# A decoder layer on one core: a reordered boundary between attention and feed-forward, additions at the turn's head, and x normalised by ScalarE

## The reference

```python
x = x + attn(layernorm(x))                    # 8 query heads, 2 key/value heads, rope, causal
x = x + wkv(layernorm(x), ctx)                # decayed running sums over time, per channel
x = x + h_bitlinear(silu(gate) * up, w_down)  # gate, up = h_bitlinear(layernorm(x), w)
# attn: softmax(q k^T / sqrt(32)) v, mixed per head with a second ("geometric") softmax
#       of products of the first 3 channels' projections, then @ Wo
# wkv:  y_t = (sum_s w^(t-s) e^k_s v_s + e^(u+k_t) v_t) / (the same without v)
# h_bitlinear: Hadamard transform, per-token 8-bit rounding, ternary weights, matmul
```

## Time and profile before

| | us |
|---|---|
| median of 3 runs (431.3, 433.52, 435.24) | 433.52 |
| the profiled execution | 436.28 |
| its span, first to last instruction | 434.5 |
| rounds 4 to 15 of attention | 67 to 231 |
| first z of pair 0, of pair 1, of pair 3 | 258.33, 278.02, 319.94 |

### The profile page before, as it was taken

The page is one execution under the profiler, slowest core; times in us unless marked ns, Lnnn a source line. Parts: engine busy times, 40 slices in busy tenths (PEclk is TensorE's granted clock), DMA queues, the critical chain, the costliest instruction groups (busy, mean ns, idle before and its releaser), DMA issues. The chain is left out here.

```text
span 434.5 us, 7685 instructions
## 1 busy us (share of the span) xinstructions
PE 359.6 (83%) x2338; PEld 252.4 (58%) x2338; DVE 341.9 (79%) x936; ACT 269.2 (62%) x534; POOL 130.6 (30%) x160
## 2 busy tenths in 40 slices
PE   1877899889888898979888666588888999989794
PEld 1644555565555655555555344476767777778573
DVE  4473989888899888988897647788879889897732
ACT  1242767668776687757687535766848576675542
POOL 1201232334324343232341223432424343332310
PEclk9965999999999999998999978698999999999999
DMA  8960003000000000000000000000000000000001
GB/s 220 296 217 2 0 2 109 14 14 14 2 12 14 14 13 2 12 14 14 14 2 13 14 0 0 2 2 0 14 13 13 12 14 12 26 1 26 14 24 37
DMA packets 13711, 13.43 MB, mean 31 GB/s; under 512 B 2007, under 2 KB 12887, under 8 KB 13543
## 3 DMA queue, kind: packets, MB, share of 16 engines
q1 hardware_dynamic: 13671, 12.94, 10.0%
HBM read 10.84 MB, written 2.10 MB: 30 GB/s over the span
## 5 line engine op out<-in xcount | busy, mean ns | idle before, releaser
L412 POOL TENSOR_TENSOR c_h_lo<-c_hb,c_h_hi 128x512 fp32r<-128x512 f32 x32 | 41.0, 1280 | 72.9 <-ACT c_h_hi L464 67.6
L700 PE MATMUL wide<-had,c_h_hi 128*128 128x512 f32 x128 | 54.1, 423 | 8.1 <-ACT c_q2T L475 8.1
L700 PE MATMUL wide<-had,c_h_lo 128*128 128x512 f32 x128 | 51.2, 400 | 0.0
L927 PE MATMUL bank<-w_o,a_att 128*128 128x256 f32 x128 | 33.5, 407 | 13.1 <-DVE a_att L1226 12.4
L685 PE MATMUL wide<-c_q_T,w_tern_all 128*128 128x256 bf16 x256 | 37.2, 287 | 7.7 <-DVE c_hh L1038 6.1
L457 ACT ACTIVATE c_sl<-c_z 128x512 f32<-128x512 f32 x32 | 20.1, 629 | 29.8 <-DVE c_z L1029 29.7
L390 POOL TENSOR_TENSOR b_ev_in<-b_e_in,b_vT 128x256 f32<-128x256 f32 x16 | 19.9, 1242 | 50.0 <-ACT b_e_in L518 50.0
L927 PEld LDWEIGHTS bank<-w_o,a_att 128*128 128x128 f32 x128 | 24.2, 198 | 18.1 <-DVE a_att L1226 14.4
L685 PEld LDWEIGHTS wide<-c_q_T,w_tern_all 128*128 128x128 bf16 x256 | 24.2, 103 | 18.0 <-DVE c_hh L1038 8.0
L378 POOL TENSOR_TENSOR a_qk<-a_rot_c,a_rot_s 128x320 f32<-128x320 f32 x16 | 15.2, 949 | 62.5 <-DVE a_rot_s L1172 62.5
L700 PEld LDWEIGHTS wide<-had,c_h_hi 128*128 128x128 f32 x128 | 24.6, 193 | 15.0 <-issue 10.2
(11 more groups left out here) (186 smaller groups left out, 1003.0 us busy)
## 6 DMA issues: line engine op xcount, KB each, us to landing
x_res<-in_x SPq DMA_DIRECT2D x4, 512.0 KB, 7.8
b_vT<-in_ctxT SPq DMA_DIRECT2D x16, 128.0 KB, 2.3
out<-c_yo SPq DMA_DIRECT2D x16, 128.0 KB, 1.7
w_raw_all<-in_wg SPq DMA_DIRECT2D x1, 1024.0 KB, 9.2
w_raw_all<-in_wu SPq DMA_DIRECT2D x1, 1024.0 KB, 11.3
w_raw_all<-in_wd SPq DMA_DIRECT2D x1, 1024.0 KB, 13.7
had_f<-in_h SPq DMA_DIRECT2D x1, 1024.0 KB, 4.9
w_o_raw<-in_Wo SPq DMA_DIRECT2D x4, 128.0 KB, 6.1
```

What stands on the lines that cost most here:

```text
L412: nc.gpsimd.tensor_tensor(h_lo[p][:, j::FQ, :], hb[j % 2][:, :].rearrange("c (m t) -> c m t", m=2), h_hi[p][:, j::FQ, :].bitcast(F32), ALU ...
L700: mm = nc.tensor.matmul(wide[:, 1 + i, m * 512:(m + 1) * 512], a[p][:, j + FQ * m, i * P:(i + 1) * P], had512[:, j, :], start=(j == 0 and ...
L927: mm = nc.tensor.matmul(wo_o, att[p][:, i * P:i * P + P], w_o[:, i, :], start=(i == 0), stop=(i == REP - 1))
```

## The change

- `woven` runs rounds 0 to 18, then pair 1, pair 2, `finish()`, pair 3 and so on. Round 19 is gone; its scans of batch 15 stand at the head of pair 2 on VectorE, its sums and y(14), y(15) in finish().
- xn of the attention leaves VectorE. For four batches at once VectorE writes x_neg = -mean, POOL multiplies it with rstd to x_shift, and ScalarE makes xn = rstd * x + x_shift at the end of its round, one batch ahead (it gets a round -1 for xn(0)).
- On VectorE x2, x1 and the statistics of a round move to the head of the next, behind the scans: x2 is that of batch g = r - 5, x1 and the statistics those of batch c = r - 3. bxn(c) moves behind max(m).
- Pair 1's own first steps move into the rounds: pair_stats(1) behind att(15) and y(13) on VectorE, POOL's normal(1) behind round 17, ScalarE's normed(1) at the end of round 17 and turned(1) at the end of round 18, PE's turn_x(1) at the end of round 17; transformed(1) stands behind the first gate of pair 0. PE's turned_back(0) moves ahead of wo(15).
- On ScalarE the inverse of the wkv step (ln, exp) for batches 12 and 13 moves behind attention's, and that for 14 and 15 into finish(). The table set is loaded once, in finish(), where it was loaded before rounds 18 and 19.
- VectorE's part of pair 1 has a new order: z0, z1, h0, z2, h1, pair_scale, z3, h2, h3.

```diff
-def woven(attention, pair, late=None):
+def woven(attention, pair, finish=None):
-    for r in range(NB + 2):
+    for r in range(NB + 3):
         attention(r)
     pair(1)
-    attention(NB + 2)
     pair(2)
-    if late:
-        late(NB - 2)
-    attention(NB + 3)
-    pair(3)
-    if late:
-        late(NB - 1)
-    for r in range(4, NP + 3):
+    if finish:
+        finish()
+    for r in range(3, NP + 3):
         pair(r)
...
 # POOL, deviation(g)
+                    pool.wait_ge(A["mneg"], g + 1)
+                    pool.wait_ge(A["rstd"], g + 1)
+                    nc.gpsimd.tensor_tensor(x_shift[:, 4 * g:4 * g + 4], x_neg[:, 4 * g:4 * g + 4], rstd[:, 4 * g:4 * g + 4],
+                                            ALU.mult).then_inc(A["shift"], 1)
 # POOL, attention(r)
                     body(*slots(r, NB, 5))
+                    if r == NB + 1:
+                        normal(1, 1)
...
 # ScalarE, body: the inverse
-                    if d is not None:
...
+                    if d is not None and m is not None:
+                        context_inverse(*d)
...
+                    if d is not None and m is None and d[0] < NB - 2:
+                        context_inverse(*d)
 # ScalarE, end of body
+                    if e is not None:
+                        u, p = e
+                        need(act, A["t1"], u - 1)
+                        if u % 4 == 0:
+                            act.wait_ge(A["shift"], u // 4 + 1)
+                        nc.scalar.activation(xn[p][:, :], x_res[:, u, :], ACT.Identity, scale=rstd[:, u:u + 1],
+                                             bias=x_shift[:, u:u + 1]).then_inc(A["xn"], 1)
 # ScalarE, attention(r)
-                    if r >= NB + 2:
-                        nc.scalar.preload_act_table_set("natural_log_exp_and_others")
                     if r == NB:
                         turned(0, 0)
-                    body(*slots(r, NB, 5))
+                    body(*slots(r + 1, NB, 6))
...
                     if r == NB + 1:
                         channels(0, 0)
+                        normed(1, 1)
+                    if r == NB + 2:
+                        turned(1, 1)
+                def finish():
+                    nc.scalar.preload_act_table_set("natural_log_exp_and_others")
+                    for u in (NB - 2, NB - 1):
+                        context_inverse(u, u % 2)
...
 # PE, context_out
-                        need(pe, D["yo"], 2 * (u - NB + 1))
+                        need(pe, D["yo"], 2 * (u - NB + 2))
 # PE, body
+                    if b is not None and b[0] == NB - 1:
+                        turned_back(0, 0)
                     if b is not None:
...
                         mm.then_inc(A["wo"], 1)
-                    if b is not None and b[0] == NB - 1:
-                        turned_back(0, 0)
                     if d is not None and d[0] < NB - 2:
                         context_out(*d)
+                    if b is not None and b[0] == NB - 1:
+                        turn_x(1, 1)
 # PE, feed
                         gate_up(*m, 0)
+                    if f is not None and f[0] == 1:
+                        transformed(*f)
...
 # VectorE, statistics(g)
+                    nc.vector.tensor_scalar(x_neg[:, 4 * g:4 * g + 4], mv[:, 4 * g:4 * g + 4, 0], -1.0, None,
+                                            ALU.mult).then_inc(A["mneg"], 1)
 # VectorE, body
-                def body(e, f, m, b, c, d):
+                def body(e, f, m, b, c, d, g):
                     if d is not None:
+                        scans(*d)
+                    if g is not None and g[0] < NB - 2:
+                        context_add(*g)
+                    if c is not None:
+                        u, p = c
+                        need(dve, A["wo"], u + 1)
+                        need(dve, B["yt"], u - 1)
+                        nc.vector.tensor_tensor(x_res[:, u, :], x_res[:, u, :], wo_o, ALU.add).then_inc(A["x1"], 1)
+                    if c is not None:
...
+                    if m is not None:
...
+                                                AX.X, ALU.max).then_inc(A["mx"], 1)
                     if c is not None:
...
                         nc.vector.tensor_scalar(bxn[p][:, :], x_res[:, u, :], bmv[p][:, 0:1], brstd[p][:, :],
                                                 ALU.subtract, ALU.mult).then_inc(B["xn"], 1)
...
                     if d is not None and d[0] < NB - 2:
                         context_now(*d)
+                    if b is not None and b[0] == NB - 1:
+                        pair_stats(1, 1)
...
-                        nc.vector.tensor_scalar(xn[p][:, :], x_res[:, u, :], mv[:, u, 0:1], rstd[:, bass.ds(u, 1)],
-                                                ALU.subtract, ALU.mult).then_inc(A["xn"], 1)
...
-                    if d is not None and d[0] < NB - 2:
-                        context_add(*d)
-                    if b is not None:
...
 # VectorE, feed
+                    if f is not None and f[0] == 1:
+                        gated(*m, 0)
+                        gated(*m, 1)
+                        hidden(*m, 0)
+                        gated(*m, 2)
+                        hidden(*m, 1)
+                        pair_scale(*f)
+                        gated(*m, 3)
+                        hidden(*m, 2)
+                        hidden(*m, 3)
+                        return
...
+                def pair(r):
+                    if r == 2:
+                        scans(NB - 1, (NB - 1) % 2)
+                    feed(*slots(r, NP, 4))
+
+                def finish():
+                    denominator(NB - 1, (NB - 1) % 2)
+                    context_now(NB - 2, NB % 2)
+                    numerator(NB - 1, (NB - 1) % 2)
+                    context_now(NB - 1, (NB - 1) % 2)
```

More of the change, by code:

```diff
@@ L186, in decoder_layer @@
             rstd = ph.enter_context(nc.sbuf_tensor("a_rstd", [P, NB], F32))
+            x_neg = ph.enter_context(nc.sbuf_tensor("a_neg", [P, NB], F32))
+            x_shift = ph.enter_context(nc.sbuf_tensor("a_shift", [P, NB], F32))
             dq = sa("a_dq", [P, 4 * H * 3])
@@ L235, in decoder_layer @@
             yt = bank[1][:, C:2 * C]
-            names = ("st6 mv ve rstd xn t1 xT proj rot qk v hi lo dq dir tq qT s mx rows mrow grow stk hl cmx ghl "
+            names = ("st6 mv ve mneg rstd shift xn t1 xT proj rot qk v hi lo dq dir tq qT s mx rows mrow grow stk hl cmx ghl "
                      "rab gm gd sT nm es geo eg pd pn vn ln inv att wo x1").split()
@@ L415, in feed @@
                 def feed(f, m, h, b):
-                    if f is not None:
+                    if f is not None and f[0] > 1:
                         normal(*f)
@@ L665, in attention @@
                         channels(0, 0)
-                woven(attention, lambda r: feed(*slots(r, NP, 4)))
+                        normed(1, 1)
[5 more added lines that the diff above has]
+                        context_inverse(u, u % 2)
+                attention(-1)
+                woven(attention, lambda r: feed(*slots(r, NP, 4)), finish)
             @block.tensor
@@ L1357, in attention @@
                         pair_stats(0, 0)
-                    body(*slots(r + 1, NB, 6))
+                    body(*slots(r + 1, NB, 7))
                     if r == NB:
                         pair_scale(0, 0)
+                def pair(r):
[7 more added lines that the diff above has]
+                    context_now(NB - 1, (NB - 1) % 2)
                 attention(-1)
-                woven(attention, lambda r: feed(*slots(r, NP, 4)), lambda u: context_now(u, u % 2))
+                woven(attention, pair, finish)
 def constants():
```

107 lines of the change are left out of this document (49 added, 58 removed).

## The result

The changed kernel takes 440.25 us (median of 4), the kernel before 432.41 in the same set. The ratio is **1.0138, 95% interval 1.0086 to 1.0189**; on the 433.52 us of the forecast that is 6.0 us more, where 2.2 less were forecast. Measured again with six more runs (experiment 13) the ratio is 1.0100, 1.0054 to 1.0146. The profiled execution took 438.26 (span 436.5), only 2.0 more than the profiled one of before.

A forecast was written before the change was run, and what follows sets the result against it. It took a loop of PE and DVE to bound the attention rounds. Terms -5.3 + 1.6 - 0.1 + 2.0 - 0.4 = -2.2 gave 431.3 us from a median of 433.52; range 426.5 to 436.5.

The forecast's parts named there:

- The attention rounds, minus 5.3: From max(3) to max(14), eleven rounds fall from 13.56 to 13.21 us each, saving 5.3 us.
- round of 13.8: The round after round 13's extra 1.27 of DVE statistics; both were to go into new idle time up to 0.2 us.
- The first rounds, plus 1.6: In the first rounds xn(4) queues behind |w| on ScalarE, making t1, the scores and max(3) 1.6 us later.
- The boundary, plus 2.0: From max(15) to pair 1's first z: pv(15) waits for x1(14), 47.2 us instead of 45.2.
- after that, minus 0.4: After pair 1's first z: fewer ScalarE table switches, a costlier finish() and reordered y steps sum to minus 0.4 us.
- The end, 0 forecast: Pairs from pair 4 on keep their 19.1 us, so no change from pair 7 to the end.
- the rivals: Five alternative totals with chances: 427.8 us (0.20), 433.4 (0.15), 436.6 (0.08), 438.3 (0.09), 425.6 (0.08).
- Rival 4: In steady rounds xn misses its cover, t1 comes 0.6 later, rounds take 13.8; 438.3 us, 1.1% slower; chance 0.09.

The follow-up runs named there:

- kernel 6: The changed kernel plus three 128x128 products on ones in TensorE's wait before wo each round; 437.32 us, 1.0061 of the kernel before.
- kernel 2: Only the boundary reordered on the kernel before, additions and xn left as before; 433.76 us, ratio 0.9980.
- kernel 14: The kernel before with only three products on ones added before wo each round; 436.40 us, ratio 1.0023.
- kernel 3: Only xn moved to ScalarE, with its scale and shift, on the kernel before; 439.08 us, ratio 1.0097.
- 4: The kernel before with only the additions up to batch 13 at the round's head and max ahead of bxn; 433.03 us, ratio 0.9924.
- kernel 16: Kernel 15 with xn back on VectorE; 431.00 us, 0.9926 of the kernel before.
- Kernel 9: The changed kernel with its last additions, x1(14) and x2(12) among them, back at the round's tail; 435.89 us, 1.0052 of the kernel before.
- 1: The kernel before with only the rounds changed: xn on ScalarE and additions up to batch 13 at the head; 435.14 us, ratio 1.0015.
- kernel 12: The kernel before with head additions (last ones at the tail) and products on ones in wo's wait and two longer waits; 430.25 us, ratio 0.9885.
- kernel 15: The changed kernel with wo's wait filled, last additions at the tail and xn ahead of |w|; 427.64 us, 0.9833 of the kernel before.
- 18: Kernel 15 with the boundary in the order of the kernel before; 427.85 us, 0.9835 of the kernel before.

## Why the prediction was wrong

**The attention rounds, minus 5.3: the step that failed.** The sum put the clock in the rounds at nothing. The earlier trace rows showed hardly a dip there, and I read this as a property of the stage. It gained nothing there: +0.2 for -5.3. The loop itself was right to 0.01 (13.22 measured, 13.21 forecast; DVE waits 0.77 for the scores, 0.9 forecast; t1 did not wait for xn in steady rounds). Undisturbed, the eleven rounds give 4.6 (146.28 in kernel 6 against 150.85; 4.3 against the 150.62 of kernel 2, which has no stretch either) and not 5.3, since two rounds with extra DVE work take 13.87 and 13.38. The three stretches on wo then cost 4.75 in the profile, the whole gain.

What I should have priced is a stretch on wo. The wait that they follow was in the rows already (0.84), and so was a stretch: the "round of 13.8" behind round 13, which I put down to the first pair's statistics, was the one at clock 0.88. In kernels 2 and 14, which have the same statistics and no stretch, that round takes 13.57 and 13.56. Nor is it the new loop that makes a stretch dear: kernel 3 pays 1.64 and 1.33 in the old one. What the change brought is more stretches on wo, three and two between these marks where before had none on it. Why, stays open.

**The part credited.** I gave the gain to xn leaving DVE and to the scans ahead of x2 together. Kernels 3 and 4 show that the first has no part in it. The Trainium skill's "ScalarE: Activation LUTs" (Rules for kernel authors), which wants such arithmetic on VectorE, I set aside for the rounds' sake; there it makes no difference (0.59 against 0.54 us a piece, rounds of 13.22 either way). In the first rounds its place in ScalarE's queue counts, 1.8 us in each of two. It lost 1.3% behind |w| and won 0.9% ahead of it, but those two pairs of kernels differ by the filling and x2(12) too, so the turn from loss to gain is not the place's alone.

**The first rounds, plus 1.6: right in mechanism, undersized.** t1(4) was released by ScalarE's xn behind |w|, as said. What the first rounds of before take at full clock, kernel 14 shows (kernel 2 has 13.78 and 12.63); below it the same two rounds of the change:

```profile
39.54:53.31 13.77, 12.64 (x90) 8.10 (x91) 12.32 (x42) 8.96 (x19) 3.10 (x5) 1.00 0.00 0
53.31:65.93 12.62, 12.28 (x94) 8.19 (x92) 10.87 (x31) 9.26 (x21) 4.28 (x6) 1.00 0.06 11
```

```profile
37.34:51.68 14.34, 11.56 (x83) 7.22 (x85) 11.80 (x42) 9.46 (x20) 3.20 (x6) 1.00 0.00 0
51.68:65.94 14.26, 11.79 (x85) 7.42 (x87) 10.71 (x29) 10.00 (x22) 4.51 (x6) 1.00 0.16 53
```

That is 0.57 and 1.64, together 2.2; against kernel 16, which has the head and x on VectorE (13.50 and 12.46), it is 2.6. The earlier of the two was held to be even and is not. The second row of the table of stretches shows a gain there only because the profile of before fell on a low clock.

**The boundary, plus 2.0: right.** pv(15) at 15.20 (15 forecast), z(0,0) 30.19 after max(15) (29.3), z(1,0) 46.83 (47.2), against 45.17 before: +1.66. The next pair loses 1.3 more and the third gains 0.4, so "after that, minus 0.4" should have been plus 0.9. Kernel 9 takes out 2.1 by moving x1(14) and x2(12), as far as one profile each can tell; the other 0.5 is what 2 shows for the reordering (87.56 against 87.09), no more than the clock's own scatter. I named x1(14) as what holds pv(15) and not x2(12), which holds it as well.

**The end, 0 forecast, plus 1.6.** The pairs keep 19.1 from pair 4 on, as they had to. Behind pair 7 the Hadamard products run at the low clock after a wait of 2.51 for q2T (407.47); before has the same wait (407.08) and the full clock. It shows in both profiles of the change, yet comes and goes over the kernels (37.8 in before, 1, 2, 9, 12, 14, 15 and 18, over 38.7 in the rest) without a relation to the edits that I can name. Its cause is open.

**The sum.** -4.6 and 4.75 for the rounds, 2.2 for the two early rounds at full clock, 2.6 for the boundary, 1.6 for the end: 6.6, against 6.0 and 4.3 by the two ratios. It comes from single profiles, so that it comes near is in part luck. Of the rivals, none had this. Rival 4 had the right sign and size (1.1%) by another mechanism, xn missing its cover in steady rounds, which the trace excludes. Why a round of 13.2 brings more stretches than one of 13.56 (19 in eight profiles, against 3 in the three of before, 2 and 3), though its TensorE is no less busy (0.895 against 0.886), is not settled.

## What to carry to other kernels

Before a gain of a few tenths per round is added up, name the products that stand on the round's loop and ask what a stretch at TensorE's low level costs there: here 1.0 to 1.7 us a time, against 0.34 won in a round. Steady rows at full clock in the kernel before don't promise that it stays so. A wait just ahead of such products can be filled with a few products on ones, which cost no time as long as they end before the wait does; whether that pays in the whole must be measured. When work goes to another engine for relief, read the order of that engine's queue at the place where it is needed soonest. When additions are moved behind a new step, find every count that a later wait needs: two of them held pv(15), and moving one bought nothing. Where two single profiles differ, compare them stage by stage with the clock beside each.

## What was not expected of the hardware

All kernels whose wait stays open have one wait of 0.84 us ahead of wo in each round. With rounds of 13.2 this went with 2 or 3 stretches at 1.2 GHz in 150 us, in eight profiles of eight, at 1.0 to 1.7 us each where wo runs in them (3.62 instead of 1.99); with rounds of 13.56 it went with 1, 0 and 2. Three products on ones in that wait left none, in nine profiles of nine. A higher mean clock is no measure by itself: kernel 12 had 0.969 and 430.4 us in the mean, kernel 15 0.957 and 428.1.
